# Where the four token tiles of a vision-tower kernel stand in its twelve-step turn: two banks with two tiles each, or four with one each

## The chip, the cores and the metric

The kernel runs on one core of a Trainium2 chip. The metric is the device time of one execution in microseconds (us), lower is better; the time given for a kernel is the median of several executions. The engines are named as in the profile: PE (TensorE, matmuls) with PEld (its weight loads), DVE (VectorE), ACT (ScalarE), POOL (GpSimd) and SP (SyncE, which here only issues transfers).

## The reference

Sixty-four images of 14 x 14 patches (12,544 tokens, width 192) go through one tower block. Cut to what matters:

```python
h = patches @ W + b                              # 768 -> 192, "tokens"
h = h + attn(layernorm(h))                       # 12 heads of 16, rotary, causal
#   weights = where(causal, erf(q k^T / 4) + 1, 0);  y = weights @ v / weights.sum(-1);  y @ Wproj.T
h = h + ffn(layernorm(h))                        # 8 routed experts, top 2, and a shared one
```

The change touches the first two lines alone, and the layernorm and its transposes that prepare the third.

## The kernel before, in words

The program has three stages, one after the other: attention (with the tokens before it and the second norm and router logits behind it), routing, experts. The first takes about the first half of the span.

The attention works on units of 392 tokens (two images, four tiles of up to 128 rows); there are 32. A software pipeline holds three units at once. One **turn** has twelve **steps** (`n` = 0 to 11), one for each pair of (image, two heads) of the current unit `u`: scores of pair `n + 1`, the weights of pair `n`, and `attend` (weights times v) of pair `n - 4` (`LAG = 4`). Around these pairs each step carries pieces for the unit behind (`has_prev`: attention output turned, projected, added, second norm, turned, router logits) and for the one ahead (`has_next`: first norm, q, k, v), and the token products of unit `u + 2` (`has_tokens`). The kinds of turns are pre, pro, first, 29 mid turns, late, last and end. Tokens are made in pre, pro, first and mid.

Every engine walks the same steps in its own queue, in the order written, and waits on semaphores:

- PE, step `n`: scores (L829 to L835), attend (L855 to L861), then the pieces: at step 3 the normed rows are transposed (L731, positions `LN1T`), `copied(LN1T)` waits until both copies are out, and the q/k products follow (L738, positions `QK`); at steps 3 and 4 q/k, at 4 and 5 v, at 4 the transposes of y, at 5 the projection (`PROJ`), at 9 the transposes of the second norm's rows (`X2T`), at 11 the router product.
- All these pieces share two PSUM banks (`NB = 2`). A piece has a **position** in the turn, and position modulo 2 is its bank. `room(pos)` makes PE wait until ACT has copied the earlier piece out of that bank; `copy_out(pos, ...)` on ACT waits until PE has filled it.
- ACT, step `n`: copy of the scores of pair `n + 1` (L418, `copy_scores`, which waits until DVE has weighed pair `n - 3`), the GELU of pair `n` (L433), then the copies (L409).
- DVE, step `n`: product of pair `n + 1` (L552), weighing of pair `n - 1` (L559), reciprocal of pair `n` (L611), the causal floor of pair `n - 1` (L567, for which `attend` of that pair waits), then the pieces: at step 0 the first norm's rows (L545), at 3 and 4 the rotary (L629 to L636), at 5 the sum of projection and residual (L652, behind `out_of(PROJ)`) and the second norm's statistics, at 6 the second norm's rows (L545), at 6 and 7 the low parts of q/k (L648), at 1 and 10 the outputs, at 11 the bias on the tokens and their statistics.
- POOL, step `n`: one product for pair `n` (L687), and the two root steps (L677) behind the statistics.
- SP: patches of a later unit after the first norm, then the transfers of v, the transposing transfers of q/k, and the stores of the second norm's rows, in a fixed order.

Of the tokens, the tiles are made by `tokens(n)`: six products of 128 x 192, printed in the profile as twelve matmuls. Two tiles share one position:

```python
    (1, 2), (3, 4, 5, 6), (7, 10), (8, 9), (11, 12), (14, 15), (17,), (0, 13))   # ..., X2T, ROUTE, TOK
...
                    pos, at = TOK[n // 2], n % 2 * D
                    out = room(pos) if n % 2 == 0 else bank[pos % NB]
```

They are issued at steps 0 and 1 (position 0) and at 7 and 8 (position 13), each behind the step's attend.

Of the kernel before, what the change touches and what calls it, by code (L numbers as in the profile page):

```python
# [72 lines left out]
class Tally:  # L73
# [24 lines left out]


LN1T, QK, VV, YT, PROJ, X2T, ROUTE, TOK = (  # L100
    (1, 2), (3, 4, 5, 6), (7, 10), (8, 9), (11, 12), (14, 15), (17,), (0, 13))
NEXT = LN1T + QK + VV
PREV = YT + PROJ + X2T + ROUTE
TURNS = {
# [10 lines left out]
NB = 2  # L115
# [131 lines left out]
def attention(nc, dram):  # L247


    with ExitStack() as ctx:  # L250
# [142 lines left out]
        @block.scalar  # L393
        def _(act):

            act.wait_ge(zero_set, 1)
            for rows in (dram["x2"], dram["out"]):
                spare = rows[N:N + SPARE, :].rearrange("n d -> (n d)").rearrange("(p z) -> p z", p=128)
                act.dma_start(spare, zeros[:]).then_inc(zeroed, 16)
            act.dma_start(dram["table"].rearrange("(v s) c -> v (s c)", s=XU), dram["empty_table"]).then_inc(zeroed, 16)  # L400

            def turn(kind, u, prior, slot):
                prev = 1 - slot
                pairs, has_next, has_prev, has_tokens = parts_of(kind)

                def copy_out(pos, dst, rows, cols=UT):

                    act.wait_ge(full[pos % NB], fills(kind, u, pos))
                    nc.scalar.copy(dst, bank[pos % NB][0:rows, 0:cols]).then_inc(free[pos % NB], 1)  # L409

                def copy_scores(u, n, opens):

                    pair = PAIRS * u + n
                    act.wait_ge(scored, pair + 1)
                    if not opens:

                        act.wait_ge(weighted, pair - 3)
                    nc.scalar.activation(x_pair[:, n % 4], score[n % 2][:, :, 0:PACKED], ACT.Copy,  # L418
                                         scale=QK_SCALE ** -2).then_inc(copied_out, 1)

                for n in range(PAIRS):
                    if pairs and n < PAIRS - 1:
                        copy_scores(u, n + 1, kind == "first" and n < 3)
                    if n == PAIRS - 1 and has_next:
                        copy_scores(u + 1, 0, kind == "pro")
                    if pairs:

                        pair = PAIRS * u + n
                        act.wait_ge(copied_out, pair + 1)
                        if kind != "first" or n >= 4:  # L430

                            act.wait_ge(attended, pair - 3)
                        nc.scalar.activation(weights[:, n % 4], x_pair[:, n % 4], ACT.Gelu, scale=SCORE_SCALE)\  # L433
                          .then_inc(gelued, 1)
                    if n == 3 and has_next:
                        for k, pos in enumerate(LN1T):
                            copy_out(pos, normed_t[:, k * UT:(k + 1) * UT], KD)
                    if n in (3, 4) and has_next:
                        for t in range(2 * n - 6, 2 * n - 4):
                            copy_out(QK[t], qk_raw[:, t, :], 128, 2 * D)  # L440
                    if n in (4, 5) and has_next:
                        pos = VV[n - 4]
                        if has_prev and n == 4:

                            act.wait_ge(held_in[prev], 32 * prior + 32)
                        act.wait_ge(full[pos % NB], fills(kind, u, pos))
                        for t in range(2):
                            last = nc.scalar.copy(v[prev][:, 2 * (n - 4) + t, :, 0:HD],
                                                  bank[pos % NB][:, t * D:(t + 1) * D]
                                                  .rearrange("p (h d) -> p h d", h=NH))  # L450
                        last.then_inc(free[pos % NB], 1)
                    if n == 4 and has_prev:
                        for k, pos in enumerate(YT):
                            copy_out(pos, y_t[:, k * UT:(k + 1) * UT], KD)
                    if n == 5 and has_prev:

                        act.wait_ge(rows_out[prev], 64 * prior + 64)
                        for k, pos in enumerate(PROJ):
                            copy_out(pos, h2[prev][:, 2 * k:2 * k + 2, :].rearrange("p t d -> p (t d)"), 128, 2 * D)
                    if n in (6, 7) and has_next:  # L460
                        if kind != "pro":

                            act.wait_ge(qk_turned[n - 6][slot], 32 * turned_uses(kind, u, prior, slot, False))
                        for t in range(2 * n - 12, 2 * n - 10):

                            act.wait_ge(qk_rotated, 4 * u + 5 + t)
                            for a, parts in ((0, slice(0, 3, 2)), (1, slice(0, 2))):
                                src = rotated[:, t, a * NH:(a + 1) * NH, :].unsqueeze(2).to_broadcast([128, NH, 2, HD])
                                nc.scalar.copy(heads_of(qk[:, t], a)[:, :, parts, :], src).then_inc(qk_hi, 1)
                    if n == 8 and has_next:  # L470
                        if has_prev:

                            act.wait_ge(spread_ready, last_root(kind, u))
                        act.wait_ge(biased, u + 2)
                        nc.scalar.copy(h[prev][:], h_new[prev][:]).then_inc(h_kept, 1)
                    if n in (1, 8) and has_tokens:
                        k = n // 8
                        copy_out(TOK[k], h_new[slot][:, 2 * k:2 * k + 2, :].rearrange("p t d -> p (t d)"), 128, 2 * D)
                    if n == 9 and has_prev:

                        act.wait_ge(x2t_out[prev], 16 * prior + 16)
                        for k, pos in enumerate(X2T):
                            copy_out(pos, x2_t[prev][:, k * UT:(k + 1) * UT], 128)
                    if n == 11 and has_prev:
                        act.wait_ge(logits_out[prev], 16 * prior + 16)
                        copy_out(ROUTE[0], logits[prev][:], E)

            turns(turn)
            act.wait_ge(zeroed, 48)

        @block.vector
        def _(dve):
# [89 lines left out]
            def turn(kind, u, prior, slot):  # L582
# [8 lines left out]
                for n in range(PAIRS):  # L591
# [48 lines left out]
                    if n in (6, 7) and has_next:  # L640

                        for t in range(2 * n - 12, 2 * n - 10):
# [3 lines left out]
                                .rearrange("p (a h x) -> p a h x", a=2, h=NH)[:, :, :, 0:HD]  # L646
                            src = rotated[:, t].rearrange("p (a h) d -> p a h d", a=2)
                            nc.vector.tensor_tensor(lo, src, hi, ALU.subtract).then_inc(roped, 1)  # L648
                    if n == 5 and has_prev:
                        out_of(PROJ)  # L650
                        dve.wait_ge(h_kept, u)
                        step(nc.vector.tensor_tensor(h2[prev][:], h2[prev][:], h[prev][:], ALU.add))  # L652
                        spread_of(1, h2[prev])
                    if n == 6 and has_prev:
                        norm(1, last_root(kind, u), h2[prev], x2[prev], x2_ready)
                    if n == 10 and pairs:
                        outputs(u, 0)
# [12 lines left out]
        def _(pool):  # L670
# [19 lines left out]
            def turn(kind, u, prior, slot):  # L690
                pairs, has_next, has_prev, has_tokens = parts_of(kind)
                for n in range(PAIRS):
                    if pairs:
                        cross(u, n, kind == "first" and n == 0)
                    if n == 11 and has_tokens:
                        root(0, token_root(u))
                    if n == 5 and has_prev:
                        root(1, last_root(kind, u))

            turns(turn)  # L700
# [2 lines left out]
        def _(pe):  # L703
# [7 lines left out]
            def turn(kind, u, prior, slot):  # L711
# [28 lines left out]

                def tokens(n):

                    pos, at = TOK[n // 2], n % 2 * D
                    out = room(pos) if n % 2 == 0 else bank[pos % NB]
                    for i in range(KP):
                        last = nc.tensor.matmul(out[:, at:at + D], wide(patches[slot], i, n), tok_w[:, i, :],  # L746
                                                start=(i == 0), stop=(i == KP - 1))
                    if n % 2:
                        last.then_inc(full[pos % NB], 1)

                for n in range(PAIRS):
                    if pairs and n < PAIRS - 1:
# [13 lines left out]
                    if n == 3 and has_next:  # L766
                        pe.wait_ge(normed_ready, 4 * u + 8)
                        transposed(LN1T, normed)
                        copied(LN1T)
                    if n in (3, 4) and has_next:  # L770
                        for t in range(2 * n - 6, 2 * n - 4):
# [12 lines left out]
                    if n == 5 and has_prev:  # L784
                        copied(YT)
                        for k, pos in enumerate(PROJ):
# [1 line left out]
                            for c in range(2):  # L788
                                last = product(out[:, c * D:(c + 1) * D], y_t, 2 * k + c, proj_w, D)
                            last.then_inc(full[pos % NB], 1)  # L790
                    if n in (0, 1, 7, 8) and has_tokens:
                        if n == 0:
                            if kind == "mid":
                                pe.wait_ge(patches_in[slot], 16 * (prior + 3 - slot))
                            else:
                                pe.wait_ge(patches_in[slot], 16 * (u // 2 + 2))
                        tokens(n if n < 2 else n - 5)
                    if n == 9 and has_prev:
                        pe.wait_ge(x2_ready, 4 * u)
                        for pos, turn_part in zip(X2T, (turn_near, turn_far)):  # L800
                            out = room(pos)
# [928 lines left out]
```

## Time and profile before

| | |
|---|---|
| median of 3 executions | 3598.76 us (3595.02 to 3599.0) |
| the profiled execution's own time | 3599.66 us |
| its span (first to last instruction) | 3597.9 us |
| PE busy | 3289.4 us, 91% |
| DVE busy | 2453.7 us, 68% |
| ACT busy | 1595.3 us, 44% |
| mean granted clock of PE | 0.916 |

The profile is of one execution. The granted clock is a share of 2.4 GHz; 0.5 is 1.2 GHz. Busy shares are means over three stages that have different limits, so the attention stage has to be read by itself. 1.8 us of the profiled execution lie outside its span.

### The profile page before, as it was taken

To read this page: it belongs to the slowest core of one execution; us is meant where nothing else is said; L and a number is where in the kernel's file an instruction comes from. 1 tells how busy PE (TensorE), PEld (TensorE's weight loads), DVE (VectorE), ACT (ScalarE), POOL (GpSimd) and SP (SyncE) were. 2 spreads that over 40 slices of the span, in tenths; PEclk is the share of its full clock that TensorE was granted. 3 is DMA by queue.
4 is the path that set the end of the run, shared out by engine and by line. 5 is a ranking of instruction groups with operands and counts; after the bars stand their busy time and mean duration, and the time that the engine had idled before them with its cause. 6 is when DMAs were issued, how large, how long until landed. Compare 5 with 4: busy or idle time off the path is not lost. (4 is left out here: it accounts for less than half of the span.)

```text
span 3597.9 us, 73107 instructions
## 1 busy us (share of the span) xinstructions
PE 3289.4 (91%) x26932; PEld 2237.2 (62%) x26932; DVE 2453.7 (68%) x4826; ACT 1595.3 (44%) x3287; POOL 1385.8 (39%) x1170
## 2 busy tenths in 40 slices
PE   6999999999999999995359999799999999999997
PEld 5677766777677777664235555566666666665665
DVE  6998999999999999996645555444444444445443
ACT  2444444444444444441024444355444444445443
POOL 1232223222222222221235552245555555555654
PEclk9899888998889889885579999999999999999999
DMA  3233233333333323331022222223323232332222
GB/s 100 70 84 71 71 71 82 84 71 64 78 82 71 75 68 82 70 57 32 33 67 70 63 74 73 80 33 62 67 37 66 36 66 39 64 64 38 43 39 30
DMA packets 330590, 227.27 MB, mean 63 GB/s; under 512 B 209103, under 2 KB 309551, under 8 KB 326159
## 3 DMA queue, kind: packets, MB, share of 16 engines
q1 hardware_dynamic: 259536, 163.94, 18.4%
q0 software_dynamic: 57472, 48.46, 9.0%
q10 hardware_dynamic: 13262, 10.65, 0.9%
q8 instruction: 195, 3.19, 0.4%
q14 instruction: 125, 1.02, 0.1%
HBM read 107.75 MB, written 67.85 MB: 49 GB/s over the span
## 5 line engine op out<-in xcount | busy, mean ns | idle before, releaser
L1268 DVE SCALAR_TENSOR_TENSOR ffn_hidden<-ffn_up,ffn_silu 128x490 f32<-128x490 f32 (+2 forms) x534 | 350.8, 670 | 780.1 <-ACT ffn_silu L1249 709.4
L687 POOL TENSOR_TENSOR weights<-weights,x_pair 128x400 f32<-128x400 f32 x384 | 395.1, 1029 | 865.5 <-DVE weights L559 765.8
L1249 ACT ACTIVATE ffn_silu<-ffn_gate 128x490 f32<-128x490 f32 (+2 forms) x534 | 302.1, 583 | 802.8 <-PE ffn_up L1212 778.4
L1420 POOL DMA_INDIRECT out_rows<-done,ids x256 | 409.7, 1601 | 508.3 <-ACT done L1524 429.4
L611 DVE RECIPROCAL recip<-x_product 128x200 f32<-128x200 f32 x384 | 534.4, 1392 | 0.0
L1233 PE MATMUL ffn_out<-ffn_w_hi,ffn_hidden_hi 128*126 128x192 f16 (+2 forms) x2124 | 530.2, 250 | 3.6 <-ACT done L1524 1.8
L1234 PE MATMUL ffn_out<-ffn_w_lo,ffn_hidden_hi 128*126 128x192 f16 (+2 forms) x2124 | 522.5, 246 | 0.4 <-issue 0.3
L1235 PE MATMUL ffn_out<-ffn_w_hi,ffn_hidden_lo 128*126 128x192 f16 (+2 forms) x2124 | 522.4, 246 | 0.0
L738 PE MATMUL bank<-w_qkv,normed_t 96*128 96x192 f32 (+1 forms) x1024 | 379.4, 531 | 42.6 <-ACT normed_t L409 42.6
L1261 DVE TENSOR_TENSOR ffn_hidden_lo<-ffn_hidden,ffn_hidden_hi 128x490 f16<-128x490 f32 (+2 forms) x534 | 356.4, 667 | 16.0
L1243 ACT CAST ffn_hidden_hi<-ffn_hidden 128x490 f16<-128x490 f32 (+2 forms) x534 | 320.9, 601 | 104.6 <-DVE ffn_hidden L1268 102.5
L1409 POOL DMA_INDIRECT tokens<-dram_x,ids x256 | 289.6, 1131 | 188.5 <-DMA ids<-dram_table 96.9
L738 PEld LDWEIGHTS bank<-w_qkv,normed_t 96*128 96x128 f32 x1024 | 224.5, 239 | 165.2 <-issue 88.7
L1233 PEld LDWEIGHTS ffn_out<-ffn_w_hi,ffn_hidden_hi 128*126 128x126 f16 (+2 forms) x2124 | 263.3, 124 | 87.5 <-issue 81.3
L433 ACT ACTIVATE weights<-x_pair 128x400 f32<-128x400 f32 x384 | 205.4, 535 | 241.4 <-PE y_sum L861 241.3
L746 PE MATMUL bank<-w_tok,patches 128*128 128x192 f32 x1536 | 287.3, 338 | 24.1 <-DVE minus_half L523 24.1
L1397 POOL DMA_INDIRECT dram_table<-entry,slot_of x196 | 202.3, 1032 | 243.9 <-issue 169.9
L855 PE MATMUL y_sum<-v_held,weights 128*64 128x68 f32 (+1 forms) x1536 | 265.2, 256 | 14.8 <-DVE weights L567 14.8
L746 PEld LDWEIGHTS bank<-w_tok,patches 128*128 128x128 f32 x1536 | 251.2, 193 | 35.1 <-issue 24.2
L1234 PEld LDWEIGHTS ffn_out<-ffn_w_lo,ffn_hidden_hi 128*126 128x126 f16 (+2 forms) x2124 | 264.2, 124 | 0.4 <-issue 0.3
L1235 PEld LDWEIGHTS ffn_out<-ffn_w_hi,ffn_hidden_lo 128*126 128x126 f16 (+2 forms) x2124 | 264.0, 124 | 0.4 <-issue 0.4
L418 ACT ACTIVATE x_pair<-score 128x400 f32<-128x400 f32 x384 | 192.5, 501 | 153.0 <-DVE weights L559 83.9
(180 smaller groups left out, 7300.3 us busy)
## 6 DMA issues: line engine op xcount, KB each, us to landing
patches<-in_patches SPq DMA_DIRECT2D x32, 1176.0 KB, 5.2
ffn_raw<-in_w SPq DMA_DIRECT2D x18, 768.0 KB
dram_x_t<-x_t SPq DMA_DIRECT2D x32, 392.0 KB, 3.5
x_t<-dram_x_t SPq DMA_DIRECT2D x24, 512.0 KB
base<-dram_h SPq DMA_DIRECT2D x24, 384.0 KB
out_rows<-sums ACTq DMA_DIRECT2D x24, 384.0 KB, 4.6
v_held<-v SPq DMA_DIRECT2D x64, 102.0 KB, 2.3
dram_h<-h SPq DMA_DIRECT2D x32, 192.0 KB
```

What stands on the lines that cost most here:

```text
L611: nc.vector.reciprocal(recip[:, n % 2], x_product[:, n % 2]).then_inc(inverted, 1)
L687: nc.gpsimd.tensor_tensor(weights[:, n % 4], weights[:, n % 4], x_pair[:, n % 4, ::-1], ALU.mult)\
L738: last = nc.tensor.matmul(out, wide(lhs, k, t), rhs[:, k, 0:width], start=(k == 0), stop=(k == 1))
L746: last = nc.tensor.matmul(out[:, at:at + D], wide(patches[slot], i, n), tok_w[:, i, :], start=(i == 0), stop=(i == KP - 1))
L1233: nc.tensor.matmul(out, hi, w_hi[:, m, :], start=(m == 0), stop=False)
L1234: nc.tensor.matmul(out, hi, w_lo[:, m, :], start=False, stop=False)
L1235: last = nc.tensor.matmul(out, lo, w_hi[:, m, :], start=False, stop=(m == MI - 1))
L1243: nc.scalar.copy(T.hidden_hi[slot][:, m, 0:n], T.hidden[:, m % 2, 0:n]).then_inc(T.hi_ready, 1)
L1249: nc.scalar.activation(T.silu[:, m % 2, 0:n], T.gate[m % 2][:, 0:n], ACT.Silu, scale=1.0 / (TOKEN_SCALE * WEIGHT_SCALE)).then_inc(T.silued, 1)
L1261: nc.vector.tensor_tensor(T.hidden_lo[slot][:, m, 0:n], T.hidden[:, m % 2, 0:n], T.hidden_hi[slot][:, m, 0:n], ALU.subtract).then_inc(T.lo ...
L1268: nc.vector.scalar_tensor_tensor(T.hidden[:, m % 2, 0:n], T.up[m % 2][:, 0:n], HIDDEN_SCALE / (TOKEN_SCALE * WEIGHT_SCALE), T.silu[:, m % ...
L1420: nc.gpsimd.indirect_dma_start(out=dram["out"][:, :], out_offset=bass.IndirectOffsetOnAxis(ap=ids[i][0:height, t, 0:1], axis=0), in_=done[ ...
```

## The change

Each token tile gets a position of its own, so each fills a bank alone and is copied out alone. The tiles move to steps 2, 3, 7 and 8; that of step 3 stands between the transposes of the normed rows and the q/k products, ahead of `copied(LN1T)`. All later positions are renumbered, which changes the bank of some pieces. The sum, statistics and root of the second norm go from step 5 to 6, its rows from 6 to 7, and its transposes on PE from 9 to 10. The same arithmetic is done.

```diff
-    (1, 2), (3, 4, 5, 6), (7, 10), (8, 9), (11, 12), (14, 15), (17,), (0, 13))
+    (1, 2), (4, 5, 6, 7), (8, 11), (9, 10), (12, 13), (16, 17), (19,), (0, 3, 14, 15))
@@ ACT
                         for k, pos in enumerate(LN1T):
                             copy_out(pos, normed_t[:, k * UT:(k + 1) * UT], KD)
+                    if n in (2, 3, 7, 8) and has_tokens:
+                        k = (2, 3, 7, 8).index(n)
+                        copy_out(TOK[k], h_new[slot][:, k, :], 128, D)
...
-                    if n in (1, 8) and has_tokens:
-                        k = n // 8
-                        copy_out(TOK[k], h_new[slot][:, 2 * k:2 * k + 2, :].rearrange("p t d -> p (t d)"), 128, 2 * D)
-                    if n == 9 and has_prev:
+                    if n == 10 and has_prev:
@@ DVE
-                    if n == 5 and has_prev:
+                    if n == 6 and has_prev:
                         out_of(PROJ)
...
-                    if n == 6 and has_prev:
+                    if n == 7 and has_prev:
                         norm(1, last_root(kind, u), h2[prev], x2[prev], x2_ready)
@@ POOL
-                    if n == 5 and has_prev:
+                    if n == 6 and has_prev:
                         root(1, last_root(kind, u))
@@ PE
                 def tokens(n):
-                    pos, at = TOK[n // 2], n % 2 * D
-                    out = room(pos) if n % 2 == 0 else bank[pos % NB]
+                    out = room(TOK[n])[:, 0:D]
...
-                    if n % 2:
-                        last.then_inc(full[pos % NB], 1)
+                    last.then_inc(full[TOK[n] % NB], 1)
...
                         transposed(LN1T, normed)
+                    if n in (2, 3, 7, 8) and has_tokens:
+                        if n == 2:
+                            ...
+                        tokens((2, 3, 7, 8).index(n))
+                    if n == 3 and has_next:
                         copied(LN1T)
...
-                    if n in (0, 1, 7, 8) and has_tokens:
-                        if n == 0:
-                            ...
-                        tokens(n if n < 2 else n - 5)
-                    if n == 9 and has_prev:
+                    if n == 10 and has_prev:
                         pe.wait_ge(x2_ready, 4 * u)
```

## Rows read from the trace of the kernel before

**Rows 1.** The page: span, busy time of each engine, granted clock in 40 slices.
```profile
span 3597.9 us, 73107 instructions
...
PE 3289.4 (91%) x26932; PEld 2237.2 (62%) x26932; DVE 2453.7 (68%) x4826; ACT 1595.3 (44%) x3287; POOL 1385.8 (39%) x1170
...
PEclk9899888998889889885579999999999999999999
```

**Rows 2.** Windows, one for each mid turn: length, busy by engine, clock.
```profile
core 0: us, PE busy (x) PEld busy (x) DVE busy (x) ACT busy (x) POOL busy (x), PEclk, DMA share, GB/s
...
762.12:814.81 52.69, 50.33 (x440) 36.70 (x440) 46.44 (x103) 23.78 (x52) 14.41 (x14) 0.87 0.34 72
...
866.80:915.54 48.74, 46.76 (x440) 35.15 (x440) 46.07 (x103) 23.75 (x52) 14.41 (x14) 0.92 0.36 77
...
963.72:1020.49 56.77, 54.55 (x441) 39.16 (x441) 48.47 (x106) 24.22 (x53) 15.45 (x15) 0.79 0.32 86
...
sum 1460.46, PE 1396.46 PEld 1034.51 DVE 1339.68 ACT 688.86 POOL 418.16; mean PE 48.15 PEld 35.67 DVE 46.20 ACT 23.75 POOL 14.42
```

**Rows 3.** Waits from 300 to 1550 us: total, times, longest.
```profile
DVE h L652 <- issue: 48.6, 25, 2.6
...
PE bank L738 <- ACT normed_t L409: 34.9, 25, 1.7
...
PE y_sum L855 <- DVE weights L567: 8.9, 24, 0.6
PE bank L731 <- ACT v L448: 8.6, 25, 0.4
```

**Rows 4.** Timeline of PE, one turn: start, length, what, idle before.
```profile
857.05 2.22 PE L746 MATMUL bank<-w_tok,patches 128*128 128x192 f32 x12
859.20 0.26 PE L829 MATMUL score<-qk_t 49*128 49x196 f16 x2
...
864.76 0.26 PE L829 MATMUL score<-qk_t 49*128 49x196 f16 x2
...
865.64 0.27 PE L855 MATMUL y_sum<-v_held,weights 128*64 128x68 f32 x1 [0.36 <-DVE weights L567]
...
866.80 1.28 PE L731 MATMUL bank<-ident,normed 128*96 128x128 f32 x8
869.37 5.09 PE L738 MATMUL bank<-w_qkv,normed_t 96*128 96x384 f32 x8 [1.29 <-ACT normed_t L409]
874.39 0.26 PE L829 MATMUL score<-qk_t 49*128 49x196 f16 x2
```

**Rows 5.** Timeline of ACT, the same turn's step 3.
```profile
867.60 0.50 ACT L418 ACTIVATE x_pair<-score 128x400 f32<-128x400 f32 x1 [2.13 <-DVE weights L559]
...
868.42 0.85 ACT L409 COPY normed_t<-bank 96x392 f32<-96x392 f32 x2
```

**Rows 6.** Timeline of DVE, the same turn.
```profile
863.06 0.37 DVE L552 SCALAR_TENSOR_TENSOR x_product<-x_pair 128x200 f32<-128x200 f32 x1
...
870.03 0.36 DVE L552 SCALAR_TENSOR_TENSOR x_product<-x_pair 128x200 f32<-128x200 f32 x1
...
872.39 0.35 DVE L552 SCALAR_TENSOR_TENSOR x_product<-x_pair 128x200 f32<-128x200 f32 x1
...
887.89 0.96 DVE L652 TENSOR_TENSOR h<-h,h 128x768 f32<-128x768 f32 x1 [1.60 <-issue]
```

**Rows 7.** Windows of PE's low clock, and one of thin work at full clock.
```profile
867.20:873.90 6.70, 5.41 (x13) 3.06 (x12) 6.63 (x13) 2.16 (x5) 2.65 (x3) 0.50 0.50 180
816.00:829.50 13.50, 12.11 (x41) 6.67 (x42) 12.88 (x27) 3.76 (x9) 3.70 (x4) 0.50 0.21 84
...
1003.70:1013.80 10.10, 10.10 (x53) 6.23 (x52) 9.81 (x26) 2.05 (x4) 3.09 (x4) 0.50 0.45 101
...
95.70:99.10 3.40, 3.40 (x55) 2.57 (x52) 3.40 (x8) 1.86 (x4) 1.02 (x1) 1.00 0.90 155
```

**Rows 8.** Timeline of PE: a token tile within such a stretch.
```profile
1009.10 4.21 PE L746 MATMUL bank<-w_tok,patches 128*128 128x192 f32 x12
```

More of the change, by code:

```diff
@@ L741, in tokens @@
                 def tokens(n):
-                    pos, at = TOK[n // 2], n % 2 * D
-                    out = room(pos) if n % 2 == 0 else bank[pos % NB]
+                    out = room(TOK[n])[:, 0:D]
                     for i in range(KP):
-                        last = nc.tensor.matmul(out[:, at:at + D], wide(patches[slot], i, n), tok_w[:, i, :],
+                        last = nc.tensor.matmul(out, wide(patches[slot], i, n), tok_w[:, i, :],
                                                 start=(i == 0), stop=(i == KP - 1))
-                    if n % 2:
-                        last.then_inc(full[pos % NB], 1)
+                    last.then_inc(full[TOK[n] % NB], 1)
                 for n in range(PAIRS):
@@ L768, in turn @@
                         transposed(LN1T, normed)
+                    if n in (2, 3, 7, 8) and has_tokens:
+                        if n == 2:
+                            if kind == "mid":
+                                pe.wait_ge(patches_in[slot], 16 * (prior + 3 - slot))
+                            else:
+                                pe.wait_ge(patches_in[slot], 16 * (u // 2 + 2))
+                        tokens((2, 3, 7, 8).index(n))
+                    if n == 3 and has_next:
                         copied(LN1T)
@@ L790, in turn @@
                             last.then_inc(full[pos % NB], 1)
-                    if n in (0, 1, 7, 8) and has_tokens:
-                        if n == 0:
[L793 to L796, printed above, removed]
-                        tokens(n if n < 2 else n - 5)
-                    if n == 9 and has_prev:
+                    if n == 10 and has_prev:
                         pe.wait_ge(x2_ready, 4 * u)
```

## The prediction

> **What bounds the kernel now.** First the page [rows 1]: PE is busy for 91% of the span, and its granted clock is 8 or 9 tenths in the first half, where the attention stage is, against nearly all 9 behind it. So before asking what a wait costs, one has to ask what the clock costs. The next view is the windows, one for each of the 29 mid turns [rows 2]. Three things are to be seen. A turn takes 50.36 us in the mean (1460.46 / 29), but not evenly: 48.7 us, 52.7 us, once 56.8 us, and the longer a turn, the lower its clock (0.92, 0.87, 0.79). PE is busy for 48.15 us of it. And DVE is busy for 46.2 us: a second engine stands only 4 us behind the first.
>
> The waits [rows 3] give PE's one large wait: the q/k products (L738) wait for ACT's copies of the turned rows, 34.9 / 25 = 1.4 us a turn. DVE's largest is 48.6 / 25 = 1.9 us a turn ahead of L652, the sum of projection and residual; the view says "issue", but the kernel has `out_of(PROJ)` there, so it is PE's projection and ACT's copies.
>
> The timelines show how these hang together in a short turn. PE starts step 3 at 864.76, waits 0.36 us for DVE's floor of step 0, turns the normed rows, waits 1.29 us, and needs 869.37 to 874.39 for four 384-column products [rows 4]. DVE begins its step 0 at 863.06 [rows 6]: PE is as far ahead of DVE as it may be. ACT's copies come only at 868.42 because ACT first stood 2.13 us at the score copy L418, which waits for DVE's weighing in step 1 [rows 5]. The turning itself was done at 868.08, 0.3 us earlier. Five steps of DVE later it is DVE that waits 1.60 us for PE [rows 6]. So one ring closes in each turn: PE from step 3 to the projection, DVE from there to the floor of the next step 0.
>
> The clock windows show the rest [rows 7]: the granted clock is 0.50 (1.2 GHz) for at least 867.2 to 873.9 in this turn and 816.0 to 829.5 in the one before, each time around the thin end of the attends, the transposes and that wait. This is why these products take 5.02 us. I take half of it, 2.5, as their length at full clock. It comes once per turn, 13.5 us instead of 6.7 in the long ones.
>
> **The two floors.** PE's work in the turn of 48.74 us, all at full clock and without waits: take off 0.36 and 1.29 [rows 4], 8.6 / 25 = 0.34 ahead of the transposes of y [rows 3], 2.5 for the products and 0.4 for the transposes (1.28 us, taken as 0.9 at full clock): 43.85 us. DVE's chain: 48.74 less its one wait, 1.60 [rows 6], is 47.1 us; busy time of 46.07 [rows 2] plus about 1 us of small steps between dependent instructions. The change touches no DVE instruction but their order, so 47.1 us is the floor of a mid turn after it.
>
> **The second norm one step on.** DVE's sum now stands behind step 5's and step 6's base work. A step without pieces takes 872.39 - 870.03 = 2.36 us [rows 6], and the low parts of q/k of step 6 are ahead of it too. Its mean wait of 1.9 us goes to nothing, the longest (2.6 us) nearly. It is not gained by itself: it lets DVE run at its 47.1. What is late next? The rows of the second norm end in DVE's step 7, and PE turns them in its step 10 instead of 9, so both move by a step; behind it PE has step 11 only to get the second turned part copied for the router product, two copies of 0.43 us each (0.85 for two in [rows 5]) against the scores and attend of a step, 866.80 - 864.76 - 0.36 = 1.68 us [rows 4]: 0, with about 0.8 us of cover. SP sends the second half of q/k behind the stores of the second norm; these are held until DVE's step 7, one step later, but PE wants that half in step 5 of the next turn. The first half is sent ahead of those stores and now comes before the norm's 2.75 us of sum and statistics, so earlier: 0, and it removes the cause of the odd 56.77 us turn if that was a late transfer. POOL's root moves with the norm, behind a product that has no hurry: 0.
>
> **Tiles on their own banks.** Twelve matmuls take 859.20 - 857.05 = 2.15 us [rows 4] wherever they stand: PE's sum is unchanged. ACT makes four copies of 192 columns instead of two of 384; ACT is busy 23.8 of 50 us, so a few tenths more are hidden by its idle time (bounds: 0 to 0.5 us of ACT, 0 on the path).
>
> **The tile between turning and products.** This should fill the 1.4 us wait. But position 3 is bank 1, the bank of the first turned part (position 1). `room` waits for ACT's first copy, and ACT is held by DVE's weighing, not by the copying. So the tile can start only one copy earlier than the products did: of 1.4 us, 0.43 us is filled and about 1.0 to 1.15 us stays whenever PE is as far ahead as now. If PE comes a microsecond later than DVE's floor, the wait vanishes by itself. Bounds: 0.4 to 1.4 us; I take 0.4 gained, 1.15 left.
>
> **The clock.** This carries most of the sum. Steps 2 and 3 now have a tile ahead of the thin end and one behind the transposes: dense work on both sides of the stretch where the clock falls. The fall need not vanish, since about 1 us of idleness plus thin attends stays. The rise is what changes: a tile in a low stretch takes 4.21 us [rows 8], and the clock was full again by the end of that stretch [rows 7], so a tile can bring it back. Behind a fall at step 3 there come now 4.2 + 5.0 = 9.2 us of dense work instead of 5.0; that 5.0 was enough in the short turns and not in the long. I expect the 13.5 us stretches to shrink to 6.7 us or less. With 6.7 us, of which some 1 us idle, PE loses about 2.85 us a turn (bounds: 0, and as now: 50.36 - 43.85 - 0.36 - 1.4 - 0.34 = 4.4 us).
>
> The Trainium skill, TensorE: Matmul & The Clock Gate, section "A second HAM failure mode: psum-queue depth-cycling", says that small idle times between groups of matmuls that cycle through PSUM banks keep the clock falling and recovering, so that work is lost at each. The trace agrees: no wait of PE here is over 1.7 us [rows 3] and the clock falls in every turn. Read by that, two more bank handovers a turn speak against this change, and the sum would be that of the rival with more falls below, 3642 us; by the rows, the q/k wait alone coincides with falls, and it gets shorter.
>
> **The sum.** PE: 43.85 + 1.15 + 0.34 + 2.85 = 48.2 us if it also has to stand as far ahead as now; but then it is later than DVE's 47.1, and up to 1.15 of it goes: between 47.1 and 48.2, I take 47.7. DVE: 47.1 plus up to 0.7 when products at low clock come late for the rotary. Both meet at 47.7 us. Per turn 50.36 - 47.7 = 2.66 us, over 29 mid turns 77 us. The late turn gains about 1 us for its norm. The pro and first turns have two tiles fewer ahead of their first products and one tile between turning and products, 2 x 1 us lost (bounds: 0 and 2 x 4.21 - 2 x 1.4 = 5.6). Together -76 us. 3599.66 - 76 = 3523.7, 3524 us. The profiled execution lies 0.9 us above the median, which I leave inside the rounding.
>
> **Rivals.**
>
> *DVE alone is the bound.* The clock does not cost PE more than 47.1 - 43.85 - 0.34 = 2.9 us. For it: the floors. Against it: PE with slack waits somewhere, and now it would wait in steps 1 to 3, in thin attends without tiles, where the clock falls. Time: 47.1 us a turn, 3.26 x 29 = 95, about 3503 us.
>
> *The change does not do what it says.* The tile waits for the same ACT copy, the falls last as long as now. Then only 0.4 us of the wait goes: PE 50.36 - 0.45 = 49.9, 13 us in all, 3586 us. For it: the bank. Against it: the tile's density behind the wait, and DVE's freed wait.
>
> *More falls: slower.* Steps 9 to 1 lose two tiles and the X2T transposes move; from the router product on, three steps run with scores and attends alone. The stretch of 1003.7 to 1013.8 [rows 7] is just such a place at low clock: 10 us until a tile brought the clock back, in the turn of 56.77, 4.1 us above its like of 52.7 [rows 2]. There is no tile at steps 0 and 1 now to end it. With a fall there in a share x of turns, the loss is 4.1 x against 2.66 gained: it decides from x = 0.65. With it in all turns: + 1.44 x 29 = 42 us, 3642 us. For it: PE has slack against DVE and must spend it in steps 1 to 3. Against it: thin steps without a wait stayed at full clock in the window of 95.7 [rows 7], and a fall that makes PE slow also takes away the wait that led to it, so it limits itself. The skill's rule quoted above would point here.
>
> **How the numbers follow.** Forecast (47.3 to 48.4 us a turn, 3504 to 3542 us): 0.50. DVE alone: 0.17. As now, with only the wait shorter, 3560 to 3595: 0.20. More falls: 0.11, counted slower. 0.02 for anything else. Range: from 3496 (DVE's floor and a few us of the edges) to 3590, which leaves out the slower case and a little of each end. A measurement of this kernel tells about 0.2%, 7 us, from no change. Faster by more: 0.50 + 0.17 + most of 0.20 = 0.83; within: 0.06; slower: 0.11.
>
> **What the profile after would show.** Mid turns between 47.1 and 48.5 us, with less spread between them. DVE's wait ahead of the sum near 0. PE's wait for `normed_t` mostly gone from L738, and one of about 1 us ahead of the token tile (L746) in its place. No low stretch of 13.5 us. PE waits for DVE's floors in steps 2 and 3, more than the present 0.36 us. The prediction is wrong if low stretches begin in steps 9 to 1 in many turns, if DVE waits for q/k at the rotary by more than 0.7 us a turn, or if the step after the second norm's transposes waits on ACT.

## The result, and the profile after

The changed kernel takes 3579.03 us in the median of 10 executions (3576.28 to 3586.03) against 3598.86 us for the kernel before; the ratio is 0.9944, with a 95% interval of 0.9929 to 0.9958. Forecast were 76 us less; it is 20 us less. The direction held and the time lies inside the range, but only a quarter of the gain came.

The page of the changed kernel, span, busy times and granted clock, to be held against [rows 1]:

```profile
span 3575.3 us, 73171 instructions
...
PE 3256.7 (91%) x26932; PEld 2254.1 (63%) x26932; DVE 2458.0 (69%) x4826; ACT 1591.8 (45%) x3351; POOL 1387.3 (39%) x1170
...
PEclk9999988999889998875579999999999999999999
```

The work is the same and the clock only a little better. The windows of the mid turns, as in [rows 2]:

```profile
258.82:306.70 47.88, 45.52 (x444) 35.29 (x441) 45.42 (x102) 23.29 (x54) 14.16 (x14) 0.96 0.37 78
...
801.44:852.59 51.15, 48.00 (x443) 37.53 (x440) 47.28 (x104) 23.89 (x55) 14.82 (x15) 0.90 0.34 75
...
900.54:952.33 51.79, 50.47 (x444) 37.90 (x441) 48.32 (x105) 24.34 (x55) 15.46 (x15) 0.84 0.38 87
...
sum 1435.21, PE 1364.87 PEld 1049.68 DVE 1341.16 ACT 684.92 POOL 417.48; mean PE 47.06 PEld 36.20 DVE 46.25 ACT 23.62 POOL 14.40
```

The mean turn is 1435.21 / 29 = 49.49 us, 0.87 less than before: 25.2 us over 29 turns. The span shrank by 22.6, so the edges cost 2.6 us, against about 1 forecast. Twelve turns take 47.8 to 48.0 us, near the forecast 47.7. The other 17 take 48.7 to 51.8 us: (1435.21 - 12 x 47.88) / 17 = 50.6. Even the twelve are not at full clock (0.96): each holds one low stretch of 3.4 us. Eleven of the others hold 6.8 to 13.7 us at low clock, and six (about 51.0 or 51.8 us, clock 0.83 or 0.84) hold one stretch of 17.1 us. So there are two things to explain: why the good turns stop at 47.88 and do not reach 47.1, and why most turns are not good.

The waits of the changed kernel, 300 to 1550 us, as in [rows 3]:

```profile
DVE x_product L552 <- ACT x_pair L418: 47.6, 25, 2.8
PE y_sum L854 <- DVE weights L567: 38.4, 40, 2.5
...
PE bank L745 <- ACT normed_t L409: 14.7, 25, 1.1
```

DVE's wait ahead of the sum (1.9 us a turn) is gone, and one of the same 47.6 / 25 = 1.9 us stands ahead of L552. PE's wait for the turned rows is 0.6 us and ahead of the tile. PE now waits 38.4 us for DVE's floor, against 8.9 [rows 3]. DVE's timeline at its step 6 shows the first:

```profile
1071.93 0.37 DVE L552 SCALAR_TENSOR_TENSOR x_product<-x_pair 128x200 f32<-128x200 f32 x1 [1.37 <-ACT x_pair L418]
...
1075.53 0.94 DVE L652 TENSOR_TENSOR h<-h,h 128x768 f32<-128x768 f32 x1
```

And ACT's timeline shows what DVE waited for, the score copy that stands right behind the two copies of the projection:

```profile
1069.63 0.48 ACT L409 COPY h<-bank 128x384 f32<-128x384 f32 x1 [0.81 <-PE bank L738]
1070.87 0.48 ACT L409 COPY h<-bank 128x384 f32<-128x384 f32 x1 [0.77 <-PE bank L738]
1071.32 0.50 ACT L418 ACTIVATE x_pair<-score 128x400 f32<-128x400 f32 x1
```

The sum at 1075.53 no longer waits, but L552, ahead of it in the same step, needs ACT at the same moment as the sum did before.

The second thing is the clock. PE's timeline around steps 1 to 3:

```profile
1044.70 0.27 PE L854 MATMUL y_sum<-v_held,weights 128*64 128x68 f32 x1 [1.59 <-DVE weights L567]
1046.30 3.43 PE L745 MATMUL bank<-w_tok,patches 128*128 128x192 f32 x12
1049.67 0.26 PE L828 MATMUL score<-qk_t 49*128 49x196 f16 x2
1051.21 0.90 PE L731 MATMUL bank<-ident,normed 128*96 128x128 f32 x8
1053.21 2.22 PE L745 MATMUL bank<-w_tok,patches 128*128 128x192 f32 x12 [1.11 <-ACT normed_t L409]
1055.27 2.75 PE L738 MATMUL bank<-w_qkv,normed_t 96*128 96x384 f32 x8
```

The products take 2.75 us where they took 5.09 [rows 4]: the fall at step 3 is gone in this turn. But PE, which has slack against DVE, spends it as a wait of 1.59 us in step 2, and there the clock falls (the tile takes 3.43 us instead of 2.22). In other turns it falls some 3 us earlier, still in step 2. Windows of low clock of the changed kernel, as in [rows 7]:

```profile
932.80:949.60 16.80, 16.80 (x126) 11.31 (x126) 16.51 (x38) 6.42 (x13) 6.18 (x6) 0.50 0.56 100
1045.50:1048.60 3.10, 3.10 (x17) 2.86 (x16) 2.88 (x13) 0.05 (x1) 1.10 (x2) 0.50 0.00 0
```

The first begins at the transposes of the second norm, which start at 932.62 in step 10, behind two steps of scores and attends alone, and goes on until the tile of step 2. PE is busy for all of its 16.8 us, with no wait, and had waited only once, 0.3 us, in the 28 us before. Six more stretches of 17.1 us begin in step 10 in kernels below (2 in e9, 3 in e10, 1 in e11); none of the twelve has a wait of PE in it, and all end inside a token tile.

Low stretches between the first and the last mid turn, read from the granted clock of the traces and put down to the step of PE in which they begin (number, and their time together in us), with the mean mid turn. Those of the column "steps 0 to 2" all begin in step 2:

| kernel | steps 9 to 11 | steps 0 to 2 | steps 3 and 4 | mean turn | time, us |
|---|---|---|---|---|---|
| before | 1, 10 | 1, 14 | 29, 283 | 50.36 | 3598.86 |
| changed | 6, 102 | 23, 123 | 4, 14 | 49.49 | 3579.03 |
| e1 norm only | 0 | 1, 14 | 29, 300 | 51.28 | 3622.86 |
| e2 tokens only | 0 | 24, 154 | 7, 24 | 48.57 | 3545.64 |
| e3 split tile | 0 | 1, 14 | 29, 197 | 51.17 | 3619.54 |
| e4 filled step | 0 | 1, 14 | 29, 195 | 51.17 | 3620.92 |
| e5 early scores | 0 | 28, 137 | 9, 48 | 49.22 | 3564.43 |
| e6 later tiles | 0 | 29, 154 | 4, 14 | 49.03 | 3559.67 |
| e7 early and later | 0 | 29, 150 | 8, 27 | 49.26 | 3563.67 |
| e8 interleaved | 0 | 25, 113 | 1, 20 | 47.77 | 3525.01 |
| e9 free DVE | 2, 34 | 3, 20 | 20, 96 | 48.01 | 3523.19 |
| e10 interleaved, norm | 3, 51 | 25, 106 | 1, 14 | 48.89 | 3570.41 |
| e11 free, interleaved | 1, 17 | 23, 99 | 0 | 47.72 | 3523.07 |
| e12 and later tiles | 0 | 26, 106 | 1, 3 | 47.74 | 3517.73 |

The times are medians of 4 to 6 executions, each beside the kernel before on the same chip (3596.2 to 3599.1 us); the turns and low stretches are of one profiled execution each. Two of these were not near the median: e9's took 3532.95 us (the slowest of five) and e10's 3555.98 us.

### The profile page after: what moved, and what is told of

Its sections match the earlier page's. It is cut to its first block and busy times, and to the rows that moved or that the text cites. A ratio compares the mean times of both kernels' runs of the same rounds, so it can differ in the third digit from the quotient of the medians.

```text
span 3575.3 us, 73171 instructions
## 1 busy us (share of the span) xinstructions
PE 3256.7 (91%) x26932; PEld 2254.1 (63%) x26932; DVE 2458.0 (69%) x4826; ACT 1591.8 (45%) x3351; POOL 1387.3 (39%) x1170
## 5 line engine op out<-in xcount | busy, mean ns | idle before, releaser
L745 PE MATMUL bank<-w_tok,patches 128*128 128x192 f32 x1536 | 340.4, 381 | 40.8 <-DVE minus_half L523 24.1
L745 PEld LDWEIGHTS bank<-w_tok,patches 128*128 128x128 f32 x1536 | 302.1, 224 | 57.2 <-issue 27.6
L738 PE MATMUL bank<-w_qkv,normed_t 96*128 96x192 f32 (+1 forms) x1024 | 272.4, 415 | 0.7 <-ACT normed_t L409 0.7
L856 PE MATMUL y_sum<-v,weights 128*64 128x51 f32 (+2 forms) x1536 | 256.4, 251 | 0.0
```

The source lines that it names most:

```text
L745: last = nc.tensor.matmul(out, wide(patches[slot], i, n), tok_w[:, i, :], start=(i == 0), stop=(i == KP - 1))
```

## The experiments

### One part alone (e1, e2)

e1 is the kernel before with (comments added here, "..." between places):

```diff
-                    if n == 5 and has_prev:      # DVE: sum, statistics; POOL: root
+                    if n == 6 and has_prev:
...
-                    if n == 6 and has_prev:      # DVE: rows
+                    if n == 7 and has_prev:
...
-                    if n == 9 and has_prev:      # ACT, PE: X2T
+                    if n == 10 and has_prev:
```

> Only the second norm is moved one step on (sum, statistics and root to step 6, rows to 7, transposes to 10); the tokens stay at steps 0, 1, 7, 8 in two banks. Theory A (the clock now falls in the steps thinned by the change: 9 and 10, which lost the second norm's transposes to step 10, and 0 and 1, which lost the tokens): the fall at step 3 stays as before in every turn, falls in steps 0 to 2 are absent, some turns fall at steps 9 to 10; 3590 to 3615 us. Rival B (what limits the new kernel is only DVE, which waits at step 6 for ACT's score copy behind the projection's copies): DVE's wait ahead of the sum turns into one ahead of L552, 0.5 us shorter, and the time is 3583 to 3592 us.

e2 is the changed kernel with these lines put back.

> Only the four token tiles are moved and given a bank each; the second norm stays at steps 5, 6 and 9. Theory A: no falls in steps 9 and 10 (the low stretches of 17 us are gone), falls in steps 0 to 2 stay; DVE waits some 2 us at the sum again, so short turns are about 48.3 us; mean turn 49.0 to 49.6, 3565 to 3585 us. Rival B (the norm's move gave what was gained): near the kernel before, 3592 to 3600 us.

e1: 3622.86 us, ratio 1.0067 (1.0050 to 1.0085). e2: 3545.64 us, ratio 0.9854 (0.9834 to 0.9875). So the change is two things in one: the tiles alone gain 53 us, and the norm's move, added to them, loses 33 us of it (3579.03 - 3545.64). DVE's waits in e1, and below them that of e2:

```profile
DVE x_product L552 <- ACT x_pair L418: 69.4, 36, 3.1
DVE by_cos L629 <- ACT qk_raw L409: 19.4, 23, 1.4
```

```profile
DVE h L652 <- issue: 36.8, 26, 2.2
```

The norm's move made DVE wait 69.4 us for ACT's score copy in that stretch. Before, it waited 48.6 us ahead of the sum [rows 3] and 9.8 us for score copies, 58.4 us together. Falls in e1 stayed at step 3, as theory A said, but none began in steps 9 and 10, where it wanted some; the time is above both forecasts. e2 had no long stretches, as theory A said, but its time is 19 us below that forecast: a turn without low clock takes 46.89 us, not the 48.3 expected. Rival B (the norm's move is the gain) is refuted.

### Filling the thin steps (e3, e4)

e3 (split) and e4 (filled), on the changed kernel, in PE's steps 1 and 2 (cut, comments added; the wait for the patches moves to step 1 as well):

```diff
+                        if n == 1:
+                            tokens(0, 0, 3)        # e3: products 0 to 2; e4: tokens(0, 3), thrown away
-                        tokens((2, 3, 7, 8).index(n))
+                        elif n == 2:
+                            tokens(0, 3, KP)       # e3; e4 makes the whole tile here
```

> As the changed kernel, but the first three products of the first tile are issued at step 1 and the other three at step 2, into the same bank; same work. Theory A: PE's idle time in step 1 is partly filled and the thin stretch shorter, so fewer than half of the falls between steps 11 and 2 are left; the long stretches from steps 9 to 10 stay in part; mean turn 48.6 to 49.2, 3555 to 3570 us. Rival B: no change, 3575 to 3583 us.

> As the changed kernel, with 1.1 us of extra work: at step 1 the first three products of the first tile are made and thrown away, and at step 2 the whole tile is made. PE does more and has the more dense steps 1 and 2. Theory A: the clock is worth more than the work; falls between 11 and 2 become rare, time at or under the changed kernel's, 3550 to 3580 us. If PE's work as such counts and not the clock: 1.1 us x 29 = 32 us slower than the changed kernel, 3610 us. Rival B: 3575 to 3585 us.

Both missed: ratio 1.0060 (1.0044 to 1.0076) and 1.0065 (1.0048 to 1.0081). The falls between 11 and 2 did vanish, all but one. But each turn fell at step 3 instead. e3's windows by turn:

```profile
623.75:674.95 51.20, 47.03 (x441) 36.09 (x441) 46.47 (x103) 23.43 (x54) 14.42 (x14) 0.93 0.31 74
674.95:726.15 51.20, 47.02 (x440) 36.06 (x441) 46.47 (x103) 23.43 (x54) 14.41 (x14) 0.93 0.30 74
```

and PE's timeline in step 3:

```profile
827.39 0.27 PE L859 MATMUL y_sum<-v_held,weights 128*64 128x68 f32 x1 [2.27 <-DVE weights L567]
828.55 1.21 PE L731 MATMUL bank<-ident,normed 128*96 128x128 f32 x8
830.70 4.21 PE L745 MATMUL bank<-w_tok,patches 128*128 128x192 f32 x12 [0.94 <-ACT normed_t L409]
834.70 3.29 PE L738 MATMUL bank<-w_qkv,normed_t 96*128 96x384 f32 x8
```

The wait moved on to step 3 (2.27 us), and the low stretch lies on the tile and the products, which DVE and ACT want at once. The low time is less than in the changed kernel (211 against 239 us), yet the time is 40 us more: where a low stretch lies matters more here than how long they are together. The reading that fits is that in step 2 it falls into PE's slack against DVE, while at step 3 it delays what ACT and DVE want next: DVE's wait for ACT ahead of L552 is 64.8 us in e3 against 47.6, and that for the q/k copies 22.2 us against 0.4. e4's 1.1 us of extra work a turn is free (3620.92 against 3619.54 us), so PE's work as such is no bound there.

### Where DVE's wait comes from (e5, e9)

e5, on the changed kernel: scores of pair 7 and their copy ahead of the projection (and skipped at step 6).

```diff
+                    if n == 5 and pairs:           # PE, ahead of PROJ
+                        scores(kind, u, 7, qk_t[slot])
...
+                    if n == 5 and pairs:           # ACT, ahead of PROJ's copies
+                        copy_scores(u, 7, False)
```

> The changed kernel, but the scores of pair 7 are made in PE's step 5 ahead of the projection, and ACT copies them ahead of the projection's copies; same work. Theory C (moving the second norm's sum one step on did not free DVE, because DVE's next instruction, L552 of step 6, needs a score copy that stands in ACT's queue behind the same projection's copies): DVE's wait ahead of L552 (1.9 us a turn) goes to under 0.3 us, DVE's sum has its cover, and turns without a low clock fall from 47.85 to 46.5 to 47.0 us; 3540 to 3560 us. Rival D (the wait comes from PE's length as such, and DVE will wait elsewhere): turns without low clock stay at 47.8, 3575 to 3585 us.

e5: 3564.43 us, ratio 0.9902 (0.9885 to 0.9918). DVE's wait at L552 is gone, and in its place stands another in the same step:

```profile
DVE qk L650 <- ACT qk L474: 41.2, 25, 2.4
```

These are ACT's casts, which stand behind the projection's copies too. Rival D was right about the length of a turn (its shortest are again 47.9 us); the time lies between the two forecasts. e9 moves the casts of step 6 to step 5 as well:

```diff
-                    if n in (6, 7) and has_next:   # ACT, now ahead of PROJ's copies
+                    if n in (5, 7) and has_next:
```

> The changed kernel with the scores of pair 7 early as in the run before, and also ACT's first two casts of q/k moved from its step 6 to step 5, ahead of the projection's copies; same work. Theory C2 (everything that DVE wants in its step 6 stands in ACT's queue behind the projection's copies, so that moving the sum to step 6 frees nothing): DVE's waits for ACT in step 6 (1.65 to 1.9 us a turn) go to under 0.4 us and turns without low clock come down from 47.85 to 46.5 to 47.0 us; 3535 to 3555 us. Rival D (another wait takes its place once more): 47.8 us and 3560 to 3580 us.

e9: 3523.19 us, ratio 0.9798 (0.9785 to 0.9811): 56 us less than the changed kernel and 12 us below what theory C2 expected. The windows of its profiled execution, which was the slowest of the five:

```profile
112.38:157.53 45.15, 44.03 (x443) 33.66 (x440) 43.78 (x99) 23.03 (x53) 13.42 (x13) 1.00 0.33 75
...
1121.74:1169.56 47.82, 45.71 (x442) 35.34 (x441) 46.15 (x103) 23.41 (x54) 14.46 (x14) 0.96 0.34 79
```

DVE's waits for ACT in step 6 are 4.4 us (casts) and 2.3 us (scores) in all 25 turns. Turns of 45.1 to 45.6 us at full clock alternate with some of 49 us; from 787 us on all turns but the last are 47.82 us long, with a low stretch of some 3 us on the tile of step 3. The short turns are cut at PE's step 3 and are made up by the next one; DVE cannot do one in 45.1 us (see below).

### The long stretches (e6, e7)

e6 puts the third and fourth tile at steps 8 and 9 (`(2, 3, 8, 9)` for `(2, 3, 7, 8)` in the changed kernel), e7 does so in e5.

> The changed kernel with its third and fourth tile at steps 8 and 9 instead of 7 and 8, so that step 9 is dense again. Theory A2 (the low stretches of 17 us begin in steps 9 and 10 because moving the second norm's transposes thinned them): these stretches are gone and the mean turn falls from 49.49 to 49.0 or less; 3560 to 3570 us. Rival (a turn always falls somewhere, and it locks on another place): 3575 to 3625 us, with one place of fall in all turns.

> Both of the two edits before: scores of pair 7 early, tiles at steps 2, 3, 8, 9. Theories A2 and C: turns without low clock at 46.5 to 47.0 and no long stretches; 3520 to 3545 us. Rival (fall at step 3 in every turn): 3590 to 3620 us.

e6: 3559.67 us, ratio 0.9895 (0.9880 to 0.9910), 19 us less than the changed kernel, with none of its six stretches of 17 us. That is what theory A2 expected, but e5 has none either with its tiles left at steps 7 and 8, so the tile at step 9 is not shown to be what took them away. e7: 3563.67 us, 0.9905 (0.9891 to 0.9919): no better than e5; its expectation (3520 to 3545) missed, because e5's half of it did.

### The bank (e8, e10)

e8 is e2 with the second tile between the two turned parts, in the bank that is free; ACT's copies follow the same order (left out here):

```diff
-    (1, 2), (4, 5, 6, 7), (8, 11), (9, 10), (12, 13), (16, 17), (19,), (0, 3, 14, 15))
+    (1, 3), (4, 5, 6, 7), (8, 11), (9, 10), (12, 13), (16, 17), (19,), (0, 2, 14, 15))
...
-                        transposed(LN1T, normed)
+                        transposed(LN1T, normed, (0,))
...
                         tokens((2, 3, 7, 8).index(n))
...
+                        transposed(LN1T, normed, (1,))
```

> Tokens only, the second norm as before; and the second tile stands between the first and the second turned part of the normed rows, in the other bank (positions 1 and 3 turned, 2 the tile), so it needs no copy first. Theory E (the tile had to wait for ACT's first copy of a turned part in the same bank): PE's wait ahead of the tile (14.5 / 25 = 0.6 us a turn) goes and some 0.5 us is left ahead of the q/k products; the falls between +2 and +6 us, which came in a quarter of the turns, are gone; 3525 to 3545 us. Rival: the slack moves to steps 1 to 3 and each turn falls there, 3545 to 3560 us.

e8: 3525.01 us, ratio 0.9806 (0.9791 to 0.9821), 21 us less than e2, at the fast end of what theory E expected. But for one of 20 us in the last mid turn, no fall begins at step 3 any more (7 in e2). PE's timeline there has one wait, behind the tile:

```profile
591.75 0.55 PE L733 MATMUL bank<-ident,normed 128*96 128x128 f32 x4
592.14 2.16 PE L747 MATMUL bank<-w_tok,patches 128*128 128x192 f32 x12
594.14 0.51 PE L733 MATMUL bank<-ident,normed 128*96 128x128 f32 x4
595.27 2.82 PE L740 MATMUL bank<-w_qkv,normed_t 96*128 96x384 f32 x8 [0.62 <-ACT normed_t L409]
```

PE's wait has changed its place and not its size: 16.1 / 26 = 0.62 us a turn ahead of the products, where e2 had 14.5 / 25 = 0.58 ahead of the tile. What did get smaller is the low clock (178 to 133 us) and DVE's wait ahead of the sum (36.8 to 18.7 us). e8 changes the bank and the order of turning and tile together; no run separates them.

e10 is e8 with the norm one step on.

> The interleaved tile of the run before, with the second norm one step on as in the change. Theory C (the norm's move costs by itself): 15 to 35 us slower than the 3525 us of the interleaved kernel, 3540 to 3560 us, with DVE waiting ahead of L552 1.5 us or more a turn. Rival (the loss of the norm's move came only through the place of the falls): 3520 to 3535 us.

e10: 3570.41 us, ratio 0.9925 (0.9908 to 0.9941), 45 us more than e8. Its executions lie in two groups, near 3556 and near 3571 us, and the profiled one is of the first. In it three stretches of 17 us are back and the shortest turn is 48.2 us instead of 47.3; DVE's wait ahead of the product of step 6 is 35.9 / 25 = 1.4 us a turn. The norm's move costs in this kernel too, by more than the 15 to 35 us expected.

### All of it (e11, e12)

e11 is e9 with e8's interleaving; e12 has also the tiles of e6.

> Interleaved tile, second norm one step on, scores and casts early. If C2 and E both hold, the two gains add: turns at 46.5 to 47.5 us, 3500 to 3520 us. If DVE's freed wait only turns into more idle time of PE in steps 0 to 3 and more falls: 3525 to 3545 us.

> As the one before with the third and fourth tile at steps 8 and 9. Theory A2: no falls begin in steps 9 and 10; the time is that of the one before or up to 10 us less. Rival: a fall locks at another place and it is slower by 10 us or more.

e11: 3523.07 us, 0.9797 (0.9784 to 0.9811). e12: 3517.73 us, 0.9788 (0.9775 to 0.9802). The gains of e8 and e9 do not add: turns settle at 47.8 us, each with a low stretch of 3.4 us in step 2, and PE waits 1.3 to 1.4 us a turn for DVE's floor. e11 missed the forecast for added gains (3500 to 3520) by 3 us; e12 is as theory A2 expected.

What stops them is DVE itself. These are all of DVE's waits for other engines over 0.15 us in e12, 300 to 1550 us:

```profile
DVE den L578 <- PE y_sum L868: 2.3, 1, 2.3
DVE x_product L556 <- ACT x_pair L418: 0.2, 1, 0.2
```

So a turn of 47.77 us is DVE's own chain, 0.7 us longer than the 47.1 worked out. The timeline has the difference, in step 6 and, for comparison, in step 7:

```profile
656.12 1.85 DVE L652 TENSOR_TENSOR qk<-rotated,qk 128x384 f16<-128x384 f32 x2
656.34 1.22 POOL L691 TENSOR_TENSOR weights<-weights,x_pair 128x400 f32<-128x400 f32 x1 [2.97 <-ACT weights L433]
...
663.10 1.01 DVE L652 TENSOR_TENSOR qk<-rotated,qk 128x384 f16<-128x384 f32 x2
```

A low-part instruction (L652) takes 0.55 us, but 1.38 to 1.39 us where it begins while POOL's product runs: 25 times in e12, 23 in e11, and never otherwise. No low part begins so in the kernel before, the changed one or e9. So the work that DVE does for a turn is the same and its length is not.

Each of e8, e9, e11 and e12 beats both kernels; their intervals overlap, so which is best is not told. For the same reason, the norm one step on with both pieces of ACT early (e11, 3523.07 us) is not shown to be better than the norm left where it was (e8, 3525.01 us).

## Why the prediction was wrong

*What bounds the kernel, the ring, the two floors.* Right in kind. DVE is what a turn cannot go below: in e9, where its waits are nearly gone, a short turn and the long one behind it are (45.15 + 49.3) / 2 = 47.2 us, against the 47.1 worked out. But 47.1 is no constant of the work: "no DVE instruction but their order" left out what runs beside it, and in e11 and e12 DVE's chain is 47.77 us.

*The second norm one step on: "Its mean wait of 1.9 us goes to nothing."* This step failed. I checked that the sum would have cover, and not what DVE does ahead of it. In step 6 L552, and behind it the casts' consumer L648, wait for ACT, whose queue is held by the same two copies. The wait kept its size in the changed kernel (47.6 us against 48.6); alone (e1) the move cost 24 us, with the tokens (e2 against the changed kernel) 33 us, and in e10 45 us. So of the 55 us by which the forecast missed, 33 go with this step. e5 and e9 together show the cause of the wait: with one held piece ahead of those copies the other takes its place, with both it falls to (4.4 + 2.3) / 25 = 0.3 us a turn, and the time is 56 us less. How much of the 56 us is that wait, and how much is low clock that came to lie elsewhere, is not separated; and no run has ACT's new order with the norm left at step 5, so the 56 us are not the worth of the norm's place.

*X2T to step 10.* I costed it as 0 by ACT's cover, and that held. What it did to the clock was counted only under the rival: six stretches of 17.1 us. Their turns are 51.4 us in the mean, 3.5 us above a good one, 21 us in all, and e6, with a tile at step 9 and without such stretches, is 19 us faster. All kernels that have them (changed, e9, e10, e11) have the moved transposes; but e1, e3 to e7 and e12 moved them too and have none, so it is at most a condition. What sets them off is open.

*Tiles on their own banks, and the tile between turning and products.* Right in kind: the tile waits for ACT's copy, 0.6 us a turn against 1.15 taken; 1.11 us was seen in one turn above. In e8, with the tile in the free bank, it does not wait, which fits the bank as the reason; the wait then stands ahead of the products, and the 21 us came with less low clock, not with less waiting.

*The clock.* I had the fall at step 3 getting shorter, and it did (283 to 14 us). I had it remain at step 3; instead 23 falls begin in step 2, behind steps 0 and 1 that had lost their tiles, where PE now idles. And the stretches that were to be 6.7 us or less are 17.1 us in six turns. This is near the rival "more falls", though that had them begin in steps 9 to 1: x = 17 / 29 = 0.59 of the turns are longer, at a price of 50.6 - 47.9 = 2.7 us each, not the 4.1 taken from one turn. It came beside the forecast gain and not in its place, so the sum lies between the two. My argument against it, that thin steps at full clock had no falls in [rows 7], left out that PE would be waiting in them: 38.4 us instead of 8.9.

The Trainium skill, TensorE: Matmul & The Clock Gate, "A second HAM failure mode: psum-queue depth-cycling", warns of small idle times between groups. The traces agree where PE waits in steps 2 and 3, all under 3 us. But PE does not wait at all in the 16.8 us window above, and only 0.3 us in the 28 us before it, so idle time is not needed for such a fall.

*The sum.* Forecast 2.66 us a turn; measured 0.87. Of the 1.79 missing, 47.88 - 47.7 = 0.18 are in what all turns take, and the rest, 17 x 2.7 / 29 = 1.6, in the longer turns: 0.7 in the six with a stretch of 17.1 us, 0.9 in the eleven others. So by turns nearly all that is missing is the clock term, which was mis-sized; by experiments 33 of 55 us go away when the norm stays where it was (e2). These are two views of one loss, not two losses: without DVE's wait in step 6 the turns and their low stretches come out differently too. Two small slips in the prediction's numbers change nothing here: 47.3 us a turn gives some 3512 us and not 3504, and the rival "DVE alone" 3505 or 3506 and not 3503.

Open is why a kernel settles where it does. e3 and e4 run into turns of 51.20 us with the clock falling at one place, (64.8 + 22.2) / 24 = 3.6 us above what DVE's chain needs; e11 and e12 settle on DVE's chain; e5 and the changed kernel have a repeating row of turns instead. No run here separates what picks the one or the other, so a time within a per cent cannot be forecast from the order of the work alone.

## What to carry to other kernels

Before a stall is moved along an in-order queue, list every instruction between the old and the new place and what each waits for: here two of them waited for the same two copies through ACT's queue, and the stall stayed. Where two engines are nearly level, slack given to one comes back as idle time at the point where it is furthest ahead; if the clock falls there, ask which work the low stretch will lie on, since in e3 it cost 40 us more on work that others want at once than in the changed kernel. A piece set into a gap should not need the resource whose release ends the gap. And an engine's chain is a floor only for the neighbours that it was measured with: look at what will run beside each of its instructions after a move.

## What the runs showed of the hardware that was not expected

Turns can settle at one length to a hundredth of a microsecond with a clock fall at the same place of each, although the work would allow a shorter one: 51.20 us in e3 and e4, where DVE waits 3.6 us of it. (The 47.8 us of e9, e11 and e12 are not of this kind: in their settled turns DVE waits for other engines some 0.5 us in e9 and not at all in e11 and e12.) Adding 1.1 us of useless matmuls to each turn changed nothing there (e4 against e3). And the granted clock (0.50, so 1.2 GHz) stayed low for 16.8 us with PE busy in all of it, in attends and small products, and rose again during the next tile of 192-column products, as at the end of all twelve such stretches. Last, the DVE instruction that begins while POOL's product runs takes 1.39 us instead of 0.55 (e12); in e5 and e7 it is 0.78 us, begun later beside the same product. In all 108 cases it ends 0.41 us behind POOL's instruction.
